# Expert stages of an eight-stage kernel: rows gathered block by block through an inverted row index, results stored in row order

## The reference, cut to what matters

```python
logits = x @ Wr + br                      # 8 experts
idx = jnp.argmax(logits, axis=-1)
gates = take_along_axis(softmax(logits), idx)
for ei in range(8):
    h = gelu(xf @ W1[ei] + b1[ei])        # 256 -> 1024
    y = h @ W2[ei] + b2[ei]               # 1024 -> 256
    out = out + y * (gf * (idxf == ei))[:, None]
# second stage: top_k(logits, 2), gates = softmax of the two, otherwise the same
x = x + out                               # input of the stage is layernorm(x)
```

## Time and profile before

| | |
|---|---|
| median of 3 runs | 2816.24 us (2816.24, 2799.23, 2816.45) |
| profiled execution | 2813.1 us, span 2811.3 us |
| mean granted TensorE clock | 0.767 |
| busy: PE, DVE, ACT, POOL | 72%, 59%, 39%, 36% of the span |
| first expert stage, l0f | 220.5 to 517.3 us |
| second expert stage, l2f | 1205.4 to 1672.2 us |

### The profile page before, as it was taken

One profiled execution on the slowest core, in us unless ns is written; L12 is line 12 of the kernel. 1 busy time (PEld: TensorE's weight loads), 2 busy tenths in 40 slices (PEclk: granted clock), 3 DMA queues, 4 the chain that ended last, 5 costly groups with the idle time before them and its releaser, 6 DMA issues. The chain is left out here.

```text
span 2811.3 us, 41872 instructions
## 1 busy us (share of the span) xinstructions
PE 2037.6 (72%) x13025; PEld 1632.3 (58%) x13025; DVE 1657.5 (59%) x5348; ACT 1097.2 (39%) x3087; POOL 1003.1 (36%) x1053
## 2 busy tenths in 40 slices
PE   6983788499159869834989907777777777763995
PEld 4653788399138756534888805555555555542663
DVE  5763000388962258640101138999999999935773
ACT  3551222355021125411322206666666666610443
POOL 3312222400000056224222245666666666504440
PEclk9995899755569979957999956676667666556997
DMA  2112554410000011124354230000000000000112
GB/s 84 63 62 74 210 181 171 127 28 1 0 34 1 12 34 62 63 101 166 112 175 139 94 97 8 8 9 8 1 8 8 1 1 1 1 6 23 36 46 72
DMA packets 99753, 163.61 MB, mean 58 GB/s; under 512 B 19774, under 2 KB 78038, under 8 KB 91606
## 3 DMA queue, kind: packets, MB, share of 16 engines
q1 hardware_dynamic: 77112, 79.62, 8.9%
q0 software_dynamic: 22464, 81.83, 8.3%
HBM read 191.23 MB, written 39.35 MB: 82 GB/s over the span
## 5 line engine op out<-in xcount | busy, mean ns | idle before, releaser
L546 DVE MATCH_REPLACE8 l3a_left<-l3a_top,l3a_left 128x256 f32<-128x256 f32 x768 | 310.0, 413 | 0.0
L539 DVE MAX8 l3a_top<-l3a_left 128x8 f32<-128x256 f32 x768 | 287.1, 417 | 0.0
L357 POOL TENSOR_TENSOR l3a_prob<-l3a_expd,l3a_rest 128x512 f32<-128x512 f32 x128 | 162.5, 1269 | 230.6 <-ACT l3a_rest L437 230.5
L264 PE MATMUL l3a_psT<-all_ident,l3a_prob 128*128 128x128 f32 x512 | 124.0, 388 | 162.2 <-POOL l3a_prob L357 162.2
L282 PE MATMUL l3a_psO<-l3a_probT,l3a_vp 128*128 128x128 f32 x1024 | 214.5, 375 | 28.8 <-ACT l3a_probT L453 28.8
L282 PEld LDWEIGHTS l3a_psO<-l3a_probT,l3a_vp 128*128 128x128 f32 x1024 | 184.1, 269 | 81.2 <-ACT l3a_probT L453 47.9
L264 PEld LDWEIGHTS l3a_psT<-all_ident,l3a_prob 128*128 128x128 f32 x512 | 83.8, 197 | 185.6 <-POOL l3a_prob L357 185.2
L344 POOL TENSOR_TENSOR l3a_kept<-l3a_raw_sc,l3a_mone 128x512 f32<-128x512 f32 x128 | 163.0, 1274 | 57.7 <-ACT l3a_raw_sc L421 57.1
L1602 ACT ACTIVATE l2f_ffn_hT<-l2f_ffn_psH,l2f_ffn_wt 128x128 f32<-128x128 f32 x312 | 89.0, 368 | 229.7 <-PE l2f_ffn_psH L1557 190.4
L1557 PE MATMUL l2f_ffn_psH<-l2f_ffn_xsT,l2f_ffn_wt 128*128 128x128 f32 x1248 | 154.0, 284 | 29.6 <-DMA l2f_ffn_wt<-in_L_table,l2f_ffn_idx 28.2
L437 ACT ACTIVATE l3a_rest<-l3a_left,l3a_nmax 128x256 f32<-128x256 f32 x256 | 116.1, 502 | 150.6 <-DVE l3a_left L546 149.8
(11 more groups left out here) (492 smaller groups left out, 4749.5 us busy)
## 6 DMA issues: line engine op xcount, KB each, us to landing
l2f_ffn_xs<-slots_x SPq DMA_DIRECT2D x39, 128.0 KB
slots_y<-l2f_ffn_y SPq DMA_DIRECT2D x39, 128.0 KB
slots_x<-l2f_route_zero SPq DMA_DIRECT2D x19, 256.0 KB, 3.0
o_at<-l0a_oraw SPq DMA_DIRECT2D x16, 256.0 KB, 2.0
l0a_osum<-o_at SPq DMA_DIRECT2D x32, 128.0 KB
o_at<-l2a_oraw SPq DMA_DIRECT2D x16, 256.0 KB, 2.0
l2a_osum<-o_at SPq DMA_DIRECT2D x32, 128.0 KB
o_at<-l3f_oraw SPq DMA_DIRECT2D x16, 256.0 KB, 2.0
```

The source lines that it names most:

```text
L264: mm = nc.tensor.transpose(psT[u % 2][:, kc, e, :], prob[:, u % 4, e, kc * P:kc * P + P], ident[:])
L357: nc.gpsimd.tensor_tensor(prob[:, u % 4, :, :], expd[:, u % 2, :, :], rest[:, u % 2, :, :], ALU.subtract).then_inc(picked, 1)
L539: ins = nc.vector.max(top[:, e, eight], rows[:, e, :] if r else scores[:, e, :])
L546: ins = nc.vector.match_replace(out=rows[:, e, :], in_to_replace=top[:, e, eight], in_values=rows[:, e, :] if r else scores[:, e, :], imm_ ...
```

## The change

The three scopes of `moe` become one. The loops of the expert part are written out, with constants in every wait.

- **Row index.** Each block gets the list of the rows it holds, `take`, and the list of places its results go, `put`. They come from the slots by one-hot products: `at_r` says which place in a block a row has, `at_b` which block, weighted by the number of the row tile and by the lane. PE multiplies the two over all `KT` tiles, DVE makes the indices from the sum.
- **Rows in.** SP stores `xn` to `rows_x` in row order, four tiles a DMA. POOL gathers each block's rows by `take`, four buffers deep. Slots without a row take row 0. The zero fill and the scatters are gone.
- **Results out.** POOL scatters each block to `rows_y` by `put`, in row order; empty slots go to a spare part. After the last block SP loads `rows_y` with plain DMAs, four tiles each, and DVE adds group by group.
- **Order.** DVE works out the block table `widx` ahead of the slots, POOL asks for the first four weight tiles right after it, with `widx` itself as index. ACT reads turned tiles 0 to 3 between the two square roots.

```diff
+            for g in range(4):
+                sp.wait_ge(x_norm, 4 * (g + 1))
+                sp.dma_start(rows_x[4 * g * P:4 * (g + 1) * P, :].rearrange("(t p) d -> p t d", p=P), xn[:, 4 * g:4 * g + 4, :])\
+                    .then_inc(kept, 16)
+            for p in range(2):
+                sp.wait_ge(rows_out[p].sem, rows_out[p].base + 16 * ((NB + 1 - p) // 2))
+            for t in range(0, NT, 4):
                 for k in range(k_top):
-                    for t in range(NT):
-                        pool.indirect_dma_start(
-                            out=slots_x, out_offset=bass.IndirectOffsetOnAxis(ap=slot[:, k * NT + t:k * NT + t + 1], axis=0),
-                            in_=xn[:, t, :], in_offset=None).then_inc(scattered.sem, 16)
-                pool.wait_ge(scattered.sem, scattered.base + 16 * KT)
...
+                    n = k * NT + t
+                    sp.dma_start(yb[:, n:n + 4, :], rows_y[P + n * P:P + (n + 4) * P, :].rearrange("(t p) d -> p t d", p=P))\
+                        .then_inc(back[t // 4], 16)
...
+            for n in range(KT):
+                if n % CUT == 0:
+                    pe.wait_ge(at_set, 1 + n // CUT + 1)
+                mm = nc.tensor.matmul(invs, at_r[:, n, :], at_b[:, n, :, :].rearrange("p w b -> p (w b)"),
+                                      start=(n == 0), stop=(n == KT - 1))
...
+            stats.root(act, 0)
+            for t in range(4):
+                read_t(t)
+            stats.root(act, 1)
...
+            def gather(j):
+                if j >= 4:
+                    pool.wait_ge(b_turned, j - 3)
+                pool.indirect_dma_start(out=xs[:, j % 4, :], out_offset=None, in_=rows_x,
+                                        in_offset=bass.IndirectOffsetOnAxis(ap=take[:, j:j + 1], axis=0))\
+                    .then_inc(rows_in[j % 4].sem, 16)
+
+            def scatter(j):
+                pool.wait_ge(y_done, j + 1)
+                pool.indirect_dma_start(out=rows_y, out_offset=bass.IndirectOffsetOnAxis(ap=put[:, j:j + 1], axis=0),
+                                        in_=y[:, j % 2, :], in_offset=None).then_inc(rows_out[j % 2].sem, 16)
+
+            pool.wait_ge(widx_set, 1)
+            fetch(0, 0)
+            fetch(1, 0)
+            fetch(0, 1)
+            fetch(1, 1)
+            pool.wait_ge(kept, 64)
+            pool.wait_ge(put_set, 1)
+            for j in range(4):
+                gather(j)
+            for j in range(NB):
+                if j + 2 < NB:
+                    fetch(0, j + 2)
+                if j:
+                    scatter(j - 1)
+                    if j + 1 < NB:
+                        fetch(1, j + 1)
+                if j + 4 < NB:
+                    gather(j + 4)
+            scatter(NB - 1)
...
+            then(nc.vector.tensor_tensor(at_b1, c["iota"][:, 0:NB].unsqueeze(1).to_broadcast([P, KT, NB]),
+                                         blk[:].unsqueeze(2).to_broadcast([P, KT, NB]), ALU.is_equal))
+            then(nc.vector.tensor_tensor(at_b0, at_b1, tile_no[:].unsqueeze(2).to_broadcast([P, KT, NB]), ALU.mult))
+            nc.vector.tensor_scalar(at_b1, at_b1, c["lane"][:, 0:1], None, ALU.mult).then_inc(at_set, 1)
+            for n in range(0, KT, CUT):
+                nc.vector.tensor_tensor(at_r[:, n:n + CUT, :], c["iota"][:, 0:P].unsqueeze(1).to_broadcast([P, CUT, P]),
+                                        rank[:, n:n + CUT].unsqueeze(2).to_broadcast([P, CUT, P]), ALU.is_equal).then_inc(at_set, 1)
```

More of the change, by code:

```diff
@@ L106, in moments, with root @@
         nc.vector.reciprocal(self.rstd[:, a:z], self.std[:, a:z]).then_inc(self.done, 1)
+    def root(self, act, g):
+        nc, (a, z) = self.nc, self.tiles(g)
+        if g == 0:
+            act.wait_ge(self.eps_set, 1)
+            nc.scalar.activation(self.warm[:], self.epst[:], ACT.Sqrt)
+        act.wait_ge(self.moments_set, z)
+        nc.scalar.activation(self.std[:, a:z], self.mv[:, a:z, 1], ACT.Sqrt, bias=self.epst[:, 0:1]).then_inc(self.rooted, 1)
     def roots(self, act):
-        nc = self.nc
-        act.wait_ge(self.eps_set, 1)
-        nc.scalar.activation(self.warm[:], self.epst[:], ACT.Sqrt)
         for g in range(2):
-            a, z = self.tiles(g)
-            act.wait_ge(self.moments_set, z)
-            nc.scalar.activation(self.std[:, a:z], self.mv[:, a:z, 1], ACT.Sqrt, bias=self.epst[:, 0:1]).then_inc(self.rooted, 1)
+            self.root(act, g)
 def picked_attention(nc, name, x, ident, ones, rstd, mean, evens, scale, w, ctxT, mask):
@@ L1671, in _ @@
                         nc.vector.scalar_tensor_tensor(out=x[:, t, :], in0=yb[:, k * NT + t, :], scalar=gate[:, k, t:t + 1],
                                                        in1=x[:, t, :], op0=ALU.mult, op1=ALU.add).then_inc(added, 1)
-        for t in range(NT):
-            dma["back"][t].base += 16 * k_top
+    for p in range(2):
+        for counted in (w1_in, w2_in, rows_out):
+            counted[p].base += 16 * ((NB + 1 - p) // 2)
+    for p in range(4):
+        rows_in[p].base += 16 * ((NB + 3 - p) // 4)
@@ L2339, in program @@
         NB = moe_blocks(2)
-        slots_x = nc.dram_tensor("slots_x", (NB * P, D), F32, kind="Internal").ap()
-        slots_y = nc.dram_tensor("slots_y", (NB * P, D), F32, kind="Internal").ap()
-        dma = {"scattered": Counted(s.sem("scattered")), "fetched_w1": [Counted(s.sem(f"fetched_w1{p}")) for p in range(2)],
-               "fetched_w2": [Counted(s.sem(f"fetched_w2{p}")) for p in range(2)],
-               "back": [Counted(s.sem(f"back{t_}")) for t_ in range(NT)]}
+        rows_x = nc.dram_tensor("rows_x", (TOK, D), F32, kind="Internal").ap()
+        rows_y = nc.dram_tensor("rows_y", (P + 2 * TOK + NB * P, D), F32, kind="Internal").ap()
+        dma = {n: [Counted(s.sem(f"{n}{p}")) for p in range(q)]
+               for n, q in (("fetched_w1", 2), ("fetched_w2", 2), ("rows_in", 4), ("rows_out", 2))}
         with Scope(nc, "start") as s0:
@@ L2372, in program @@
                          rope=(t["c_cos"], t["c_sin"]))
-        moe(nc, dma, "l2f", 2, x, ident, rstd, mean, consts, t["L2_wr"], t["L2_br"], (t["L2_table1"], t["L2_table2"]), slots_x, slots_y)
+        moe(nc, dma, "l2f", 2, x, ident, rstd, mean, consts, t["L2_wr"], t["L2_br"], (t["L2_table1"], t["L2_table2"]), rows_x, rows_y)
         picked_attention(nc, "l3a", x, ident, consts["ones"], rstd, mean, t["c_even"], DK ** -0.5,
```

613 lines of the change are left out of this document (261 added, 352 removed).

## The result

The changed kernel takes **2640.61 us** (median of four runs, 2637.93 to 2651.27); beside it on the same chip the kernel before takes 2816.34 (2799.23 to 2819.95). The ratio is 0.9394, 95% interval 0.9348 to 0.9441. The forecast was 2649, range 2622 to 2700. The profiled execution after is the longest of its four, 2651.27 us, with a span of 2649.5; against the profiled 2813.1 of before that is 161.8 us less, where the sum said 164.2. Repeated later on another chip with five rounds, the two took 2645.1 and 2809.1 (0.9411, 0.9385 to 0.9436).

The account below looks back on a forecast made before the run. It took POOL's queue to bound each expert stage's start and tail, PE and weights the loop. Starts 37.4 and 19.0, loops 33.3 and 31.1, tails 31.0 and 12.4 sum to 164.2; 2813.1 less that is 2649 us, range 2622 to 2700.

Parts of the forecast that it names:

- Starts: From entry to the first expert matmul: 37.4 us less in l2f and 19.0 us less in l0f.
- The forecast's low end: One-hot passes at l2f's start: a third of the 9.5 us taken, if 16-bit outputs run faster.
- The router's gain: Ahead of the index arithmetic: the router gets its first four tiles earlier, so its chain ends some 2.8 us sooner.
- Loops: Expert loops: PE's weight waits go, blocks take 7.24 us; 33.3 us less in l2f, 31.1 us less in l0f.
- The high end of the one-hot passes: l2f's start: the passes take 14 us at 1.54 ns per element, where 9.5 us was taken.
- The downward terms: Range below the forecast: 12 us of unknown costs (passes 7, other DVE steps 5), and repeats lying 17 us apart.
- Tails: After each loop, plain loads with DVE's additions as the pace: 31.0 us less in l2f, 12.4 us less in l0f.
- weights still late: Expert loops: rows and weights share one queue, so all 54.8 us of weight waits stay; 2713 us, chance 9%.
- DVE is held by POOL's issues: Both stages' starts: four fetches beside the one-hot passes hold DVE, 8 us together; 2657 us, chance 10%.
- The rule weighed in the prediction: VectorE and GpSimd share a port pair by exclusive lock; the second is blocked for the whole instruction: 4.1 us per stage.
- code that is no longer a loop: Written-out expert loops: fetching the code costs 1 us in each of 62 blocks; 2711 us, chance 6%.
- POOL becomes the bound: Expert loops: four POOL issues per block against two; slower overall from 2.5 us per issue, 2864 at 2.7 us; chance 2%.

## Why the prediction was right, step by step

- **Starts.** Right by its mechanism. From `first` to the indices: 16.0 us where the sum had 18.45. The first two passes over `at_b` took 1.46 each (1.5 by the slope) and four of 1024 elements 4.62 (5.04). Mis-sized was the third pass over `at_b`: 0.57 for 1248 elements, not 1.5. The forecast's low end had it that 16-bit *outputs* might run faster; the first pass has a 16-bit output too and took 1.46. The third is the one whose large operands are all 16-bit and which has a single large source; no run here tells the two apart. The Trainium skill, "VectorE: DVE Perf Modes", section "The perf-mode tier table", lets a one-source operation on 16-bit data run in a faster mode; 0.57 beside 1.46 agrees. On the other side POOL issued the gather 0.78 us after `take` was set, where the sum had none of it. (The first weight fetch followed `widx`, and the last scatter its output, after 0.3; why the gather took longer isn't shown.) In l0f the gather's wait behind the weights was put at 1.3 us beyond a plain landing and was 3.8 (6.57 less 2.8). These two outweigh what the indices and the router gained, and leave l0f's start 1.1 us short of its forecast. The router's gain was 3.2 in both stages (2.8 forecast).
- **Loops.** Right: 285.89 and 169.76 against 285.5 and 169.2, every block 7.24, no wait for weights. The order alone gives it, and undoing it takes it back.
- **Range.** Two of its terms are wrong in their arithmetic. The high end of the one-hot passes is 7840 elements at 1.54 ns, 12.1 us and not 14. The downward terms, 12 and 17 us, end at 2620 and not 2622. The result lies well inside either way.
- **Tails.** Right to 0.1 us, and also in that VectorE is the pace, though by less than was thought: the loads keep just ahead of it.
- **Rival "weights still late".** It didn't happen. Its price, 2713, is near the 2719.77 of the undone order, but by luck in part: of its 54.8 us of waits only 46.7 had lain inside the loops, where 53.0 came back, and the lower clock cost 20.4 where 9 had been set. In the kernel before it cost 15.9, by the same difference of PE's busy time.
- **Rival "DVE is held by POOL's issues".** Beside the index arithmetic POOL's four issues took 1.25, 1.16, 0.99 and 1.40 us, where they take 1.0 elsewhere; the last ran beside the two passes of 1.46. The DVE passes took their slope's time. A control lies in the run with the gather first: there POOL is idle during l0f's passes, and they take the same 0.54, 0.55, 0.33 and 2.35 us as in the changed kernel, where issues of 1.35 and 1.19 run beside them. So what was stretched was POOL's side, by up to 0.4 us, off the path. The rule weighed in the prediction, the Trainium skill's "SBUF — State Buffer", "Who interferes with whom", has a condition that the prediction leaves out: it holds for VectorE in a 2-port mode, or with two SBUF inputs beside a GpSimd instruction that reads SBUF. Under that condition (the two passes of 1.46 have two inputs) a block for a whole instruction isn't seen on either side: the measurement decides.
- **Rival "code that is no longer a loop".** Nothing in the loops: 7.24 per block. (Its price of 1 us a block came from no row.) Whether it has to do with GpSimd's long end is open.
- **Rival "POOL becomes the bound".** The threshold was worked out as if the loss grew by POOL's time alone. With a fill in the place of the sixth issue it does (17 to 22 us); with a sixth transfer it costs 123. The margin is one more transfer a block, and behind it is a cliff.

## What to carry to other kernels

When a scatter by position becomes a gather by a list worked out on chip, the list's arithmetic must be shorter than the issues it replaces: 16 us of VectorE against 41 of GpSimd here. Look first at the order within one issuing engine's list, for it was worth 63 of the 164 us and needed nothing else of this change; a request for data that was free early must not stand behind one that waits for the block's output. And price a PE wait with the clock that follows it: 1.4 times its length.

## What the runs showed that was not expected

- With six indirect transfers per block ACT and DVE stall (123 us in all; the longest wait of DVE is 10.6 us where 3.4 are usual), with five the kernel stands at 2649, and with the same bytes on SyncE's queue at 2652.
- The next stage begins 6.0 to 8.4 us after GpSimd's last record where GpSimd works last, or nearly last, in the written-out stage.
- A 16-bit one-source VectorE pass took 0.57 us for 1248 elements and 0.33 for l0f's 368, so 0.27 ns more per element; the first of the two-source passes beside it took 1.46 and 0.54, 1.05 ns per element.
